# Splitting expert weights on another engine, reordered score banks and filler matmuls in an attention and expert kernel

## What is computed

```python
x = x + conv_attn(group_norm(x))       # layer 0: 12 heads of 32, with relative position terms
t = t + attn(layer_norm(t))            # layer 1: 12 heads of 32
xr = layer_norm(t)                     # the expert layer
probs = softmax(xr @ gate_w.T + gate_b)            # 8 experts
topv, topi = top_k(probs, 2); topv = topv / sum(topv)
for e in range(8):
    h = relu(xr @ w1[e].T + b1[e])                 # 384 -> 1536
    out = out + tok_w[:, e:e+1] * (h @ w2[e].T + b2[e])   # 1536 -> 384
t = t + out
```

## Time and profile before

| | |
|---|---|
| median of 3 runs | 995.97 us (995.62 to 996.94) |
| the profiled execution | 995.26 us |
| its span, first to last instruction | 993.5 us |
| mean granted TensorE clock in the span | 0.951 |
| TensorE busy | 880.6 us (89%) |
| VectorE, ScalarE, GpSimd busy | 499.3, 353.4, 322.7 us |

### The profile page before, as it was taken

One profiled execution on the slowest core, in us unless ns is written; L12 is line 12 of the kernel. 1 busy time (PEld: TensorE's weight loads), 2 busy tenths in 40 slices (PEclk: granted clock), 3 DMA queues, 4 the chain that ended last, 5 costly groups with the idle time before them and its releaser, 6 DMA issues. The chain is left out here.

```text
span 993.5 us, 17630 instructions
## 1 busy us (share of the span) xinstructions
PE 880.6 (89%) x6045; PEld 676.3 (68%) x6046; DVE 499.3 (50%) x879; ACT 353.4 (36%) x582; POOL 322.7 (32%) x191
## 2 busy tenths in 40 slices
PE   4969699999999999999999998319999999999991
PEld 3447376676776545666666645319999999999991
DVE  5323656766664345767776725602442442442424
ACT  0112044454445322355445471303342342342430
POOL 0200057777678220357576660140000000000403
PEclk9989699999999999999999999559999999999996
DMA  9474853343342003145665325631652652643214
GB/s 290 103 158 125 294 165 96 100 132 106 96 121 62 16 13 72 32 132 149 198 194 156 113 48 198 231 119 32 238 201 69 246 174 95 230 164 121 85 37 140
DMA packets 75901, 132.92 MB, mean 134 GB/s; under 512 B 14264, under 2 KB 52152, under 8 KB 75856
## 3 DMA queue, kind: packets, MB, share of 16 engines
q1 hardware_dynamic: 64688, 114.33, 38.1%
q10 hardware_dynamic: 9120, 11.74, 3.5%
q0 software_dynamic: 2048, 6.29, 2.0%
HBM read 78.81 MB, written 37.26 MB: 117 GB/s over the span
## 5 line engine op out<-in xcount | busy, mean ns | idle before, releaser
L924 DVE TENSOR_REDUCE mhalf<-ps 128x1 f32<-128x512 f32 x384 | 241.3, 682 | 117.0 <-PE ps L640 113.8
L1103 ACT ACTIVATE prob<-ps 128x1024 f32<-128x1024 f32 x192 | 190.3, 1026 | 222.0 <-PE ps L661 99.1
L541 POOL TENSOR_TENSOR qf<-qf,prob 128x1024 f32<-128x1024 f32 x79 | 188.3, 2383 | 16.2 <-POOL qf L541 8.7
L828 PE MATMUL ps<-xT,w 128*128 128x128 f32 x1440 | 165.5, 276 | 1.4 <-ACT xT L1160 1.4
L828 PEld LDWEIGHTS ps<-xT,w 128*128 128x128 f32 x1440 | 164.8, 193 | 1.8 <-issue 1.8
L640 PE MATMUL ps<-km,qm 96*128 96x512 f32 x384 | 151.4, 465 | 9.1 <-DVE mhalf L924 6.8
L651 PE MATMUL ps<-qa,ka 97*128 97x512 f32 x384 | 146.9, 425 | 7.0 <-DMA qa<-row 6.2
L640 PEld LDWEIGHTS ps<-km,qm 96*128 96x128 f32 x384 | 113.5, 320 | 38.8 <-DVE mhalf L924 24.5
L1182 ACT ACTIVATE h_f<-ps,b1c 128x128 f32<-128x128 f32 x240 | 66.7, 376 | 148.9 <-PE ps L828 148.9
L661 PE MATMUL ps<-prob,va 128*32 128x256 f32 x1536 | 107.5, 385 | 0.0
L651 PEld LDWEIGHTS ps<-qa,ka 97*128 97x128 f32 x384 | 69.6, 192 | 53.2 <-issue 26.4
(11 more groups left out here) (128 smaller groups left out, 857.9 us busy)
## 6 DMA issues: line engine op xcount, KB each, us to landing
w<-in_w SPq DMA_DIRECT2D x24, 768.0 KB, 7.3
w_raw<-in_w SPq DMA_DIRECT2D x24, 768.0 KB, 11.9
heads<-parts SPq DMA_DIRECT2D x32, 256.0 KB, 4.6
qb<-heads SPq DMA_DIRECT2D x12, 512.0 KB, 4.3
xs<-zero SPq DMA_DIRECT2D x8, 768.0 KB, 3.7
qm<-heads SPq DMA_DIRECT2D x12, 384.0 KB, 3.7
qa<-parts SPq DMA_DIRECT2D x36, 128.0 KB, 2.4
ka<-parts SPq DMA_DIRECT2D x36, 128.0 KB, 2.4
```

The lines of the kernel that those rows point to most:

```text
L541: pool.tensor_tensor(acc[b], acc[b], prob[:, n % NP, :], ALU.add).then_inc(a_ok[L], 1)
L828: last = mm(ps[:, g, c % HG * P:(c % HG + 1) * P], w1[b][:, k, c * P:(c + 1) * P], xT[:, k, :], start=(k == 0), stop=(k == KT - 1))
L924: v.tensor_reduce(mhalf[:, b, qt, half:half + 1], ps[:, MAX_BANK[i], :], AX.X, ALU.max).then_inc(mx_ok[L], 1)
L1103: act.activation(prob[:, s % NP, :], ps[:, 3 + 2 * (s % 2):5 + 2 * (s % 2), :].rearrange("p a b -> p (a b)"), ACT.Exp).then_inc(p_ok[L], 1)
```

## The change

- GpSimd splits the second-layer weights of experts 1 to 7, with 12 copies and 12 subtractions of one chunk (384 columns) an expert, between its scatter and its gather. Expert 0 is split by ScalarE and VectorE as before, ahead of the loop. `w2_hi_ok` and `w2_ok` count chunks.
- SP loads the second-layer weights ahead of the first-layer weights, from expert 1 on.
- `MAX_BANK` has another order, from which `MAX_BACK` is worked out.
- The four parts of `invert_sums` are done after the maxima of tiles 3, 5, 6 and 7 of a head, one each; before, all four were done after those of tile 7.
- `busy(n)` issues n matmuls on TensorE whose result nobody reads: 4 in each layer end, after the first two thirds of five tiles and a wait for ScalarE's copy of the last head; 2 ahead of each of the last three turned tiles of each layer; 9 ahead of the counts; 38 ahead of the first tile of the experts.

```diff
-MAX_BANK = (0, 1, 2, 0, 1, 2, 0, 1, 2, 0, 1, 2, 0, 1, 2, 1)
-MAX_BACK = (4, 2, 4, 3, 3, 3, 3, 3, 3, 3, 3, 3, 3, 3, 3, 2)
+MAX_BANK = (0, 1, 0, 1, 2, 0, 1, 0, 2, 1, 0, 1, 2, 0, 1, 2)
+MAX_BACK = tuple(next(d for d in range(1, 2 * TT + 1) if MAX_BANK[(i - d) % (2 * TT)] == MAX_BANK[i]) for i in range(2 * TT))
+INVERT = (3, 5, 6, 7)
...
+            if e < 1:
+                load_first()
             for q in range(WQ):
                 eng.dma_start(piece2(w2_raw[b], q), piece2(second, q)).then_inc(ld_1[b][WQ + q], 16)
+            if e >= 1:
+                load_first()
...
+            for e in range(1, NE):
+                b, turns = e % 2, e // 2
+                for q in range(WQ):
+                    pool.wait_ge(ld_1[b][WQ + q], 16 * (turns + 1))
+                    pool.sem_inc(pool_in, 1)
+                    for c in range(q * WC, (q + 1) * WC):
+                        pool.tensor_copy(w2_hi[b][:, c, :], w2_raw[b][:, c, :]).then_inc(w2_hi_ok[b], 1)
+                    for c in range(q * WC, (q + 1) * WC):
+                        pool.wait_ge(w2_hi_ok[b], HC * turns + c + 1)
+                        pool.sem_inc(pool_in, 1)
+                        pool.tensor_tensor(w2_lo[b][:, c, :], w2_raw[b][:, c, :], f(w2_hi[b][:, c, :]),
+                                           ALU.subtract).then_inc(w2_ok[b], 1)
...
+            def busy(n, out=ps[:, 5, 0:C], src=t[:, 0, :]):
+
+                for i in range(n):
+                    mm(out, before[:], src, start=True, stop=True)
...
                 for tt in range(5):
                     project(tt, (0, 1))
+                pe.wait_ge(vs_ok[L], NH)
+                busy(4, ps[:, 7, P:HALF], bproj[:, 0, :])
                 for i in L2:
                     pe.wait_ge(st_o[L][i], 64 * NH // 2)
...
                     if 3 <= tt < TT + 3:
+                        if tt >= TT:
+                            busy(2, ps[:, 7, P:HALF], bproj[:, 0, :])
                         turn_stream(tt - 3)
...
+            busy(9)
             pe.wait_ge(sel_ok, 1)
...
+            busy(38)
             pe.wait_ge(cum_ok, 1)
...
-                                pe.wait_ge(w2_ok[b], pair * WQ + c // WC + 1)
+                                pe.wait_ge(w2_ok[b], pair * HC + c + WC)
...
-                        if s == (TT - 1 if left else 2) and not first:
+                        if not first:
                             for part in range(4):
-                                invert_sums(h - 1, part)
+                                if s == (INVERT[part] if left else 2):
+                                    invert_sums(h - 1, part)
...
+            for q in range(WQ):
+                v.wait_ge(w2_hi_ok[0], WC * (q + 1))
+                v.tensor_tensor(piece2(w2_lo[0], q), piece2(w2_raw[0], q), f(piece2(w2_hi[0], q)),
+                                ALU.subtract).then_inc(w2_ok[0], WC)
...
-                    for q in range(WQ):
-                        v.wait_ge(w2_hi_ok[b], pair * WQ + q + 1)
-                        v.tensor_tensor(piece2(w2_lo[b], q), piece2(w2_raw[b], q), f(piece2(w2_hi[b], q)),
-                                        ALU.subtract).then_inc(w2_ok[b], 1)
...
-                if e > 0:
-                    round_second(e)
```

More of the change, by code:

```diff
@@ L314, in load_expert, with load_first @@
             first, second = (a[w][bass.ds(e, 1)].rearrange("e (k p) n -> p (e k) n", p=P) for w in ("w1", "w2"))
-            for q in range(WQ):
-                eng.dma_start(piece1(w1[b], q), piece1(first, q)).then_inc(ld_1[b][q], 16)
+            def load_first():
+                for q in range(WQ):
+                    eng.dma_start(piece1(w1[b], q), piece1(first, q)).then_inc(ld_1[b][q], 16)
+            if e < 1:
+                load_first()
             for q in range(WQ):
                 eng.dma_start(piece2(w2_raw[b], q), piece2(second, q)).then_inc(ld_1[b][WQ + q], 16)
+            if e >= 1:
+                load_first()
         def load_biases(eng, e, b):
@@ L1139, in _, with round_second @@
             act.activation(pr[:], lg[:], ACT.Exp).then_inc(act_own, 1)
-            def round_second(e):
-                b = e % 2
+            def round_second():
                 for q in range(WQ):
-                    act.wait_ge(ld_1[b][WQ + q], 16 * (e // 2 + 1))
-                    act.activation(piece2(w2_hi[b], q), piece2(w2_raw[b], q), ACT.Copy).then_inc(w2_hi_ok[b], 1)
+                    act.wait_ge(ld_1[0][WQ + q], 16)
+                    act.activation(piece2(w2_hi[0], q), piece2(w2_raw[0], q), ACT.Copy).then_inc(w2_hi_ok[0], WC)
             def load_x(start):
@@ L1163, in _ @@
                 act.wait_ge(st_o[1][i], 64 * NH // 2)
-            round_second(0)
+            round_second()
             act.wait_ge(scattered, 16 * 2 * TT)
```

## The result

Four runs of the changed kernel took 982.34 to 987.55 us, median 985.9, against 995.8 for the kernel before (four runs, 994.99 to 996.94): a ratio of 0.9895, interval 0.9864 to 0.9925. The forecast was 981.5, range 973 to 991. The profiled execution took 984.91 us, 10.35 less than that of before, where the sum gave 13.8 less.

What follows compares the result with a forecast made beforehand. TensorE was taken to set the end almost everywhere, so edits count only where it waits or gets more work. Terms -9.1 - 10.9 + 4.7 + 3.0 - 0.5 - 1.0 = -13.8 us took 995.26 to 981.5, range 973 to 991.

Steps and rivals of the forecast that it cites:

- Experts: Expert stage: seven expert changes stop costing 1.58 us each (-11.1), GpSimd holding VectorE costs 2; -9.1 us.
- Heads: Attention heads: new banks and spread reciprocals save 0.86 us in nine layer-1 heads, 0.34 in nine layer-0 heads; -10.9 us.
- End of layer 0: Layer 0's end: four fillers not hidden, +2.66 us, six ahead of turned tiles +2.0; +4.7 us.
- End of layer 1: Layer 1's end: four fillers +2.66 us, six more +1.0, half the clock fall avoided -0.7; +3.0 us.
- Routing: Nine fillers beside VectorE's choice of experts make the counts run faster; VectorE waits only 0.48 us for them; -0.5 us.
- First tile: First expert tile: 38 fillers end some 4 us early; if the clock stays up, about 2 us, half counted; -1.0 us.
- The hold: Experts: each h_hi and h_lo on VectorE may be held up to one GpSimd instruction, 1.1 us; 2 us charged in all.
- Rival (b): Experts: GpSimd holds VectorE at nearly every group, +12 us, 993.5 at worst, 988 half way; chance 0.13.
- (c): Routing: clock stays at 1.2 GHz, so the nine and 38 fillers take longer; 1010 us in full; chance 0.07 shared with (d).
- (d): Experts: TensorE waits for GpSimd's split; gain gone at 37.5 us an expert, 1024 us at 42; chance 0.07 shared with (c).
- Rival (a): Layer ends: fillers are hidden or the clock repays them, so the +7.7 falls away: 973.8 us; chance 0.15.

Runs made afterwards that it cites:

- interleaved kernel: Kernel with VectorE's remainders for expert 0 begun after the scatter, changed so each GpSimd subtraction directly follows its own copy: 983.53 us, 0.9859 of before.
- three banks in turn: Kernel after, but each layer's first 26 maxima matmuls go to banks 0, 1, 2 in turn: 983.81 us, 0.9881 of before.
- the late split: Kernel after with 46 instead of 38 fillers and GpSimd's split for expert 1 held until VectorE split the first tile's h: 987.81 us, 0.9874 of before.
- the old reciprocals: Kernel after with only the four reciprocals back behind the last tile's maxima, banks staying new: 990.19 us, 0.9934 of before.
- the last kernel: Kernel after without layer-end fillers, with first maxima cycling three banks, expert 0's remainders after the scatter, expert 1's split held back, 42 fillers: 972.68 us, 0.9753 of before.

## Why the prediction was right, and where it was short

Its terms, from the stages of before and after:

- **Experts**, -9.1 forecast: -10.3 in the 17 tiles. All seven changes of expert are gone; later holds of VectorE cost 249.5 - 248.8 = 0.7, the last figure being the interleaved kernel's, not 2.
- **Heads**, -10.9: 3.7 in layer 0 and 8.6 in layer 1, 12.3. Bank and reciprocals were sized rightly, and putting both back took 11.4 away.
- **The same banks in the values of layer 1**, not in the sum at all: +2.4. The step that failed is that the new order was judged by the head's stretches alone. In the values stage little lies between maxima, and a bank that comes again two matmuls later waits for VectorE. The run with three banks in turn took the 2.4 back.
- **End of layer 0**, +4.7: +4.46. Nothing hid the fillers.
- **End of layer 1**, +3.0: +2.26, by two wrong halves. With the clock up through the projection in both, the end takes 34.55 us with fillers and 30.43 without: they cost at least 4.1, not 3.7 (the shorter end was at half clock behind its projection, in the last gate products). And the 1.9 by which the profiled run came out cheaper was the clock, which the fillers there don't hold: with the same fillers it fell in the kernels with the late split and the old reciprocals (37.8 us), and without any it stayed up in the last kernel's projection. Two windows of each (granted clock third from the end), from the same part of that stage, of the kernel after and then of that with the old reciprocals:

```profile
607.00:609.00 2.00, 2.00 (x8) 1.18 (x8) 0.82 (x4) 0.67 (x2) 0.00 (x0) 1.00 0.41 144
609.00:611.00 2.00, 2.00 (x14) 1.58 (x13) 1.67 (x5) 0.38 (x2) 0.00 (x0) 1.00 0.00 0
```

```profile
610.00:612.00 2.00, 2.00 (x7) 1.70 (x8) 1.12 (x4) 0.67 (x2) 0.00 (x0) 0.50 0.57 199
612.00:614.00 2.00, 2.00 (x4) 1.04 (x4) 0.00 (x0) 0.00 (x0) 0.00 (x0) 0.50 0.00 0
```

- **Routing**, -0.5: -0.45, shown by leaving the nine out.
- **First tile**, -1.0: +1.6 for the tile, and +1.0 for the scatter ahead of it, which was not in the sum. The fillers end too early by 6.7 us, not 4, and the clock is down when the tokens are there. With 46 it stayed up under the first product in one traced run and fell in the other, behind waits of 1.6 and 1.4 us; no run shows a number of fillers that holds it.
- **The hold**, charged as "up to one GpSimd instruction, 1.1 us": in the first tile it was 4.0 us, through four subtractions, the last of the split for expert 1. The Trainium skill, "SBUF — State Buffer", section "Who interferes with whom", says that VectorE blocks until GpSimd's instruction is over; in this tile it was until a row of instructions was over, and the measurement decides. In the kernel after it cost only 0.28 us of waiting, since a first product at half clock in part covered it.

With +0.8 at the tail and +0.3 elsewhere these make the 10.4 us by which the span fell. That the total landed in the range is in part luck: experts, heads and layer ends came out 3.6 us better than forecast together, the values, the way to the first tile and the rest 7.1 us worse. Rival (b), that GpSimd holds VectorE, was thus right about one tile and wrong about the others; (c) and (d) did not occur: the routing is at full clock, and GpSimd needs 20.5 us where (d) put the limit at 37.5 (35 + 14/6 is 37.3). Rival (a) was wrong: leaving the end fillers out gained 6.3 us by the ratios.

What stays open: why VectorE gets in between GpSimd's instructions in later experts and not in the first split. Pauses don't decide it alone. In the eleven traces with GpSimd's uninterrupted order, the 66 later splits, too, run their 24 instructions without a gap, in 19.6 to 20.6 us, and no `h_hi` takes over 1.30 us there. Two rows of the kernel after, from its second split:

```profile
706.73 4.56 POOL L611 TENSOR_TENSOR w_lo<-w_raw,w_hi 128x384 fp32r<-128x384 f32 x4
707.27 0.77 DVE L1080 CAST h_hi<-h_f 128x512 fp32r<-128x512 f32 x1 [1.32 <-ACT h_f L1212]
```

One difference shows in the traces: when each of the 66 began, an `h_hi` or `h_lo` was running or came within 0.4 us, while a held instruction came 1.7 to 13.3 us into its split. But the late split, where `h_hi` came 7.9 us in, held VectorE in one trace of three, so this is no rule either. The early split held VectorE to its end in all eight traces that have it uninterrupted.

## What to carry to other kernels

Judge a new order of buffers in every stage that uses it, above all where little lies between two uses. Work moved to GpSimd can hold VectorE for a whole row of instructions; where VectorE must get in, let GpSimd wait for its own result between instructions, which was enough in the one kernel that tried it. A filler is free only where TensorE waits for something that lies further off than the filler is long. When a stage ahead of a covered wait is made faster, look for what was hidden under it: the first product at full clock only uncovered the hold.

## What was not expected of the hardware

- VectorE held beside GpSimd's split for 4.0, 6.5, 9.3 and 15 us (20.17 less its own 5.1), in a copy or subtraction that takes 0.43 us or 1.7 by itself; and two outcomes, 0.85 and 9.32 us, at the same distance of 0.43 us from GpSimd's block.
- The clock in the end of layer 1 falls or stays in kernels with the same code there, for 1.7 to 3.3 us, and in one trace it fell in the end of layer 0 (28.85 us instead of 27.16). The four runs of the kernel after differ in their mean clock: 0.970 at 982.34 and 984.91 us, 0.967 at 986.9 and 987.55. That this is the end of layer 1 isn't shown, since only the run of 984.91 us was traced.
- The first scatter instruction takes 1.19 us alone and 2.70 where VectorE's subtraction started 0.12 us ahead of it. Later ones take 1.15 to 1.56 us when they start while a subtraction runs, and 0.96 to 0.98 otherwise.
